# First attention of a fused two-layer kernel: batch 1's score shift, the scale transpose and the exponentials change places

## The reference

```python
x = x + L0_xattn(ln(x), ctx)    # 16 heads of 32, causal, softmax
x = x + L0_ffn(ln(x), ...)      # 8 experts, top 2, SiLU gating
x = x + L1_xattn(ln(x), ctx)    # 16 heads, low-rank queries, keys with rope
x = x + L1_ffn(ln(x), ...)      # weights and activations rounded to 8 bit
```

```python
scores = q @ k.T / sqrt(32); scores = where(causal, scores, min)
attn = softmax(scores); out = (attn @ v) @ Wout.T
```

## Time and profile before

| | value |
|---|---|
| median of 3 runs | 837.28 us |
| profiled execution, its span | 830.72 us, 828.9 us |
| PE, DVE, ACT, POOL busy, share of the span | 83%, 62%, 50%, 30% |
| mean granted TensorE clock | 0.932 of full speed |
| chain that ended last: PE, DVE, ACT, issue, DMA | 59%, 15%, 9%, 8%, 5% |

### The profile page before, as it was taken

One profiled execution on the slowest core, in us unless ns is written; L12 is line 12 of the kernel. 1 busy time (PEld: TensorE's weight loads), 2 busy tenths in 40 slices (PEclk: granted clock), 3 DMA queues, 4 the chain that ended last, 5 costly groups with the idle time before them and its releaser, 6 DMA issues.

```text
span 828.9 us, 13011 instructions
## 1 busy us (share of the span) xinstructions
PE 690.5 (83%) x4427; PEld 552.5 (67%) x4427; DVE 510.2 (62%) x1038; ACT 416.0 (50%) x777; POOL 247.3 (30%) x278
## 2 busy tenths in 40 slices
PE   0799999654999999992988988988988698799985
PEld 0587777453777777692867877878867375566542
DVE  4876677474666666538476476476475623677674
ACT  3513566363555555321377477476475522455452
POOL 2000742332122222054066166085073001122232
PEclk9987999765999999996799999999999999999997
DMA  8565842598675665698001223123257952111000
GB/s 260 192 209 145 297 147 59 185 390 302 188 228 176 188 184 162 206 297 202 12 1 50 60 50 85 42 60 77 64 172 201 387 191 70 52 52 39 13 14 28
DMA packets 82964, 118.90 MB, mean 143 GB/s; under 512 B 40769, under 2 KB 63037, under 8 KB 79329
## 3 DMA queue, kind: packets, MB, share of 16 engines
q1 hardware_dynamic: 79777, 109.71, 41.6%
q0 software_dynamic: 3136, 8.53, 4.1%
HBM read 97.15 MB, written 27.62 MB: 151 GB/s over the span
## 4 chain that ended last, share of the span: by engine, by line
PE 59%; DVE 15%; ACT 9%; issue 8%; DMA 5%; POOL 1%; ACTq 1%; SPq 0%; DVEq 0%; POOLq 0%
PE PS L149 14%; PE PS L151 12%; PE PS L150 12%; PE PS L1231 4%; PE PS L1407 3%; PE PS L1292 3%; PE PS L1589 2%; DMA raw<-wkv_in 2%; DMA yg<-ys_scratch,slots 2%; DVE nmx L1810 2%; ACT w_hi L884 1%; PE PS L1384 1%; ACT cx_hi L1119 1%; DMA cx_raw<-tile_scratch 1%; ACT wraw L973 1%
## 5 line engine op out<-in xcount | busy, mean ns | idle before, releaser
L831 POOL TENSOR_TENSOR wraw<-wraw,rinv 128x361 f32<-128x361 f32 (+1 forms) x104 | 80.9, 787 | 127.2 <-DVE rinv L1803 126.3
L1646 DVE TENSOR_TENSOR w_lo<-w,w_hi 128x1408 fp32r<-128x1408 f32 x40 | 64.9, 1623 | 39.7 <-ACT w_hi L884 39.7
L973 ACT ACTIVATE wraw<-PS,nmx 128x361 f32<-128x361 f32 (+1 forms) x104 | 58.6, 564 | 30.8 <-DVE nmx L1810 17.8
L1810 DVE TENSOR_REDUCE nmx<-PS 128x1 f32<-128x361 f32 (+1 forms) x104 | 55.1, 531 | 30.3 <-PE PS L151 30.3
L859 POOL TENSOR_TENSOR wraw<-gs,us 128x352 f32<-128x352 f32 (+1 forms) x28 | 26.7, 953 | 139.8 <-ACT gs L1147 112.2
L1813 DVE TENSOR_TENSOR pt_lo<-PS,pt_hi 128x384 fp32r<-128x384 f32 (+1 forms) x104 | 55.7, 535 | 16.3 <-ACT pt_hi L979 15.0
L884 ACT CAST w_hi<-w 128x1408 fp32r x40 | 54.7, 1369 | 18.6 <-DMA w<-w_in 9.4
L784 POOL DMA_INDIRECT xb<-xn_scratch,rows x20 | 31.8, 1589 | 106.6 <-PE PS L1203 103.5
L1407 PE MATMUL PS<-ident,wraw 128*128 128x128 f32 x312 | 52.2, 276 | 11.3 <-DVE pt_lo L1813 5.5
L149 PE MATMUL PS<-w_hi,xt_hi 128*128 128x352 f32 x160 | 56.9, 355 | 5.6 <-DVE xt_lo L1640 5.4
L149 PE MATMUL PS<-pf_hi,cx_hi 128*128 128x512 f32 (+1 forms) x112 | 48.1, 429 | 11.8 <-DVE x_tiles L2003 4.5
(11 more groups left out here) (270 smaller groups left out, 1937.1 us busy)
## 6 DMA issues: line engine op xcount, KB each, us to landing
w<-w_in SPq DMA_DIRECT2D x20, 768.0 KB, 5.5
w<-w_in SPq DMA_DIRECT2D x8, 1408.0 KB, 11.4
fq_raw<-foldq_in SPq DMA_DIRECT2D x6, 1088.0 KB, 7.8
cx_raw<-tile_scratch SPq DMA_DIRECT2D x6, 1024.0 KB, 5.1
ys_scratch<-yb SPq DMA_DIRECT2D x20, 256.0 KB, 5.5
ctx_scratch<-ctxo SPq DMA_DIRECT2D x24, 192.0 KB, 1.9
fp_raw<-foldp_in SPq DMA_DIRECT2D x7, 640.0 KB, 5.0
wraw<-wup_in SPq DMA_DIRECT2D x12, 256.0 KB, 4.3
```

Of the source, the lines that this page charges most:

```text
L831: pool.tensor_tensor(P1[slot][0:rows, 0:NK], P1[slot][0:rows, 0:NK], rinv[0:rows, jj, t:t + 1].broadcast_to((rows, NK)), ALU.mult).then_in ...
L973: act.activation(P1[t % 8][r, 0:NK], PS[r, t % 4, 0:NK], ACT.Exp, bias=nmx[r, jj, t:t + 1], accum_out=rsum[r, jj, t:t + 1]).then_inc(C["ex ...
L1646: dve.tensor_tensor(WL[which][:, :], w12_of(dve_wlo.e, which), WH[which][:, :].bitcast(F32), ALU.subtract) \
L1810: dve.tensor_reduce(nmx[r, jj, t:t + 1], PS[r, t % 4, 0:NK], AX.X, ALU.max, negate=True).then_inc(C["max"], 1)
```

## The change

There are three edits, all in the first attention's loop.

1. DVE takes the maxima of batch 1's scores and shifts them before `dve_maxima(7)`, `dve_maxima(8)` and `dve_scales()`, and no longer in `batch(0)`.
2. PE's `turn_scales` moves from `batch(0)`, ahead of pv(0), to `batch(1)`, behind ot(0) and ahead of pv(1). The wait for ACT's copy moves from the second half of pv(0) to that of pv(1), and ACT's copy `act_scale_rows` from `batch(0)` to `batch(1)`, behind `OH` of batch 0.
3. On ACT the exponentials of batch n+1 come ahead of `act_add(n-2)`, in every batch that has both (n = 2 to 6).

```diff
@@ ACT, batch(n, j)
                 if n > 0:
                     act_attn0_oh(act, n - 1)
-                else:
+                if n == 1:
                     act_scale_rows()
+                if n < B - 1:
+                    act_attn0_exp(act, n + 1, 1 - j)
                 if n >= LAG0:
                     act_add(n - LAG0)
-                if n < B - 1:
-                    act_attn0_exp(act, n + 1, 1 - j)
                 if n >= LAG0 and n % 2 == 0:
                     act_sub(n - LAG0)
@@ PE, pe_attn0_pv
-                if g == 1 and n == 0:
+                if g == 1 and n == 1:
                     pe.wait_ge(W["sc"], 4)
@@ PE, batch(n, j)
                 if not first:
                     pe_attn0_ot(pe, n - 1)
+                if n == 1:
+                    turn_scales()
                 if first:
                     pe.wait_ge(A["ksb"], 8)
-                    turn_scales()
                 pe_attn0_pv(pe, n, j)
@@ DVE
             dve_attn0_project(dve, 3 * MT0 + 3)
+            dve_attn0_max(dve, 1, 1)
+            dve_attn0_shift(dve, 1, 1)
             dve_maxima(7)
             dve_maxima(8)
             dve_scales()
@@ DVE, batch(n, j)
-                if not last:
+                if not last and not first:
                     dve_attn0_max(dve, n + 1, 1 - j)
                 if not first:
                     dve_attn0_low(dve, n - 1)
-                if not last:
+                if not last and not first:
                     dve_attn0_shift(dve, n + 1, 1 - j)
```

## The result

The changed kernel takes 843.76 us (median of 20 runs, 841.01 to 855.4), the kernel before beside it 837.9 us (median of 20, 833.93 to 846.05). Executions of one and the same kernel spread over 10 us and more, so single executions show where time goes inside a stage, and only ratios say what a kernel is worth. The profiled execution took 841.71 us, its span 839.9 us, against 830.72 and 828.9 before; the mean granted clock is 0.929 (0.932). That execution before lies 7.2 us under its kernel's median and under all 20 runs (the lowest took 833.93), the changed one 2.1 us under its own, so 11.0 us between the two profiles overstate the change.

A forecast was written before the change was run, and what follows sets the result against it. PE was taken to bound the stage, on a 10.26 us ring per batch. Terms -1.7, +1.6, +1.0, +1.2, +0.2 gave +2.3, another slow stretch (+1.6) made +3.9: 834.6 profiled, 841.2 median; range 835.0 to 846.0.

The forecast's parts named there:

- The clock swings: Rival, chance 0.20: uneven batches bring four slow stretches instead of two, or POOL starts at 95.7; + 7, 844.3 us.
- The opening: Edits 1 and 2, batch 0: pv(0) starts 1.7 us earlier, out(0) and all that follows 3.3 us earlier.
- idling and the slow stretch behind it: Opening: PE waits before pv(0), then runs at clock 0.50 from 71.94 to 82.18; edits 1 and 2 bear on this.
- the early-start rival: Rival, chance 0.17: full clock through the opening, lead 6.2, POOL at 90.2; -2.1, 835.2 us.
- POOL's start: Weights' chain behind the opening: POOL's first multiplication at 92.6 instead of 87.60, bounds 91.5 and 95.7.
- Of the 3.3 us, 1.7 are left: Batch 2: ACT's add waits for POOL's set 0, ready at 96.5, cutting the opening's lead to 1.7 us.
- An even batch is 1.0 us longer: Edit 3: ACT reaches the copy of group 0 1.58 us later, so group 3 is turned at 103.38, not 102.40.
- Batch 4: + 1.0: Edit 3's cost in batch 4, counted as + 1.0 us in the sum at the attention's end.
- The slow stretches: Two half-clock stretches behind PE's idle time, + 1.6 us each: one in batch 2 or 3, one with batches 4 and 6.
- batches 3 and 5 about 10.3: Sign to look for: these odd batches take about 10.3 us at full clock; + 0.2 us for both in the sum.
- the ring: A batch's lap in the first attention, 10.26 us: addition, PE's transposes and ACT's copy, scores, ot, pv, out, next addition.
- I carry it through at par: Behind the attention: layer norm, routing and expert loads start from its end, so its + 3.9 us passes on unchanged.

The follow-up runs named there:

- e5: Changed kernel, but POOL waits with set 3 until VectorE has rounded set 1, and exponentials come ahead of the add in batch 2 alone: 1.0029 to before.
- e4: Kernel before with edit 3 alone (exponentials ahead of the add): 1.0106 to before.
- e1: Changed kernel, but POOL waits with weight set 3 until VectorE has rounded set 1: 1.0094 to before.
- e11: Changed kernel with only set 1's weight load moved behind the store of the scale rows: 1.0083 to before.
- e9: Kernel before with edits 1 and 2, set 1's load behind the scale rows' store, POOL's set 3 waiting for VectorE's rounding of set 1: 0.9954 to before.
- e12: Kernel before with only set 1's weight load moved behind the store of the scale rows: 1.0000 to before.
- e10: e9 with edit 3 (exponentials ahead of the add) kept: 1.0047 to before.
- e8: Changed kernel with edit 3 undone and POOL waiting with set 3 until VectorE has rounded set 1: 1.0046 to before.
- e3: Changed kernel with edit 3 undone, the exponentials behind the add again: 1.0073 to before.
- e2: Kernel before with five unused multiplications put ahead of POOL's first set, making POOL late: 1.0054 to before.
- e7: Kernel before with edit 2 alone: 1.0017 to before.

## Why the prediction was right, and where it was wrong

- **Direction and size.** 841.2 was forecast from 837.28, 3.9 us slower; the medians beside each other are 5.9 us apart and the ratio says 0.8%. The time, 843.76, lies in the range, but just above the likeliest case's own (839 to 843.5), and nearer to the 844.3 of "The clock swings" than to the forecast. That rival isn't borne out for it: POOL started at 91.42 and not at 95.7, and behind the opening the profiled attention adds one slow stretch, in batch 3, and lengthens those of batches 6 and 7, where that rival has four.
- **The opening** (edits 1 and 2). Right: a lead of 3.3 us was forecast, batch 0's residual came 3.8 us earlier (openings of one code differ by over 2 us, as said under the table). DVE's order and PE's half clock from 71.7 went as written; the fall ended at 78.54, and a second followed from 82 to 85.5 (0.52), as before. But "idling and the slow stretch behind it" put the fall down to the idle time, and so did the early-start rival ("the idle 1.7 us before the slow stretch goes"): that idle time went, and the clock fell at 71.9 all the same.
- **POOL's start.** Forecast 92.6, measured 91.42, just under the bound of 91.5. The store's landing was right (83.6 against 84.10), the leg behind it 7.3 us instead of 8.93. This mattered: set 0 was ready at 95.32, just before ScalarE's add asked for it at 95.38. "Of the 3.3 us, 1.7 are left" is the term mis-sized by that; 2.9 were left (residual of batch 2, 110.63 to 107.69). With POOL one us later the wait that I had forecast is there, as e5 shows.
- **An even batch is 1.0 us longer.** Right for the wait at full clock: 11.10 against 10.26, 0.84, in batch 2, and e4 shows it without the other edits. "Batch 4: + 1.0" didn't come: batch 4 took 10.25, since ScalarE had caught up in the slow batch 3; e1 and e11, without a collision, paid in it (14.22 and 12.67).
- **The slow stretches.** Two were forecast at 1.6 us each. In the profiled execution one followed the collision in batch 3 (2.2 us), and batch 6 ran at clock 0.64. I had placed the first in batch 2, which kept clock 1.00. For batch 6, 1.2 and 1.6 were counted; batches 6 and 7 together lost 1.7, since the kernel before ran slowly there too.
- **What failed: "batches 3 and 5 about 10.3".** Batch 3 took 15.92. I had let POOL's run move against the ring and asked only who waits for POOL's results, not who shares something with POOL while it runs. VectorE's rounding of set 1 came at 111.96 before, 0.9 us behind POOL's last instruction; the lead of 2.9 us and POOL's delay of 3.8 pushed one into the other. No wait in the code joins them. Any lead of the opening is lost here, as the rounding ends with POOL's run however early it starts. Batch 3's own term was 0.1, and 3.5 us of TensorE's waiting and 2.2 of slow clock were measured. At the attention's end +3.9 was forecast and +4.4 measured, but the parts differ. The lead left after batch 2 was 2.9 and not 1.7, batch 3 with its slow stretch 5.7 and not 1.7, batch 4 nothing and not 1.0, batches 6 and 7 together 1.7 and not 2.8. That they come near the same total is luck.
- **The tail.** "I carry it through at par": the attention's end moved by 4.4 us and the profiled span by 11.0. The remaining 6.6 us lie behind the attention, where neither kernel differs, and all of it in the first feed-forward part: from the statistics of the first layer norm behind the attention to those of the next it took 230.9 us before (161.77 to 392.68, clock 0.90) and 238.0 changed (166.15 to 404.19, 0.88), and what follows took 0.5 us less. The same code took between 230.7 (e9, e12) and 245.1 us (e1) in the other kernels, so most of this can be the spread of executions; the medians are 5.9 apart, 1.5 more than the attention's 4.4. The runs don't settle which part belongs to the change.

So the cause, as far as it was taken apart: edit 3 costs about 1% in both places where it was added to a kernel without a late POOL and its collision (e4; e10 against e9). Edits 1 and 2 together, with POOL's wait on set 3, are a gain of 0.5% once POOL starts earlier (89.22 in e9, against 91.64 in e8, which differs by the load order alone), and are spent when it does not (e3, e5, e8 at 1.003 to 1.007). Losses don't add: the changed kernel has both and is at 1.008, and taking edit 3 out of it (e3) changed the ratio by less than its interval. Why they don't add the profiled batches suggest, the collision hiding batch 4's loss and a late POOL making batch 2 long without edit 3, but one execution of each is all there is.

## What to carry to other kernels

When a producer is moved, follow the whole chain that starts at it, here maxima, scales, a small store, a load, another engine's run, and ask of the last link both who waits for its results and what it runs beside in its new place. An instruction put ahead of another on a queue is only free if the idle time behind it is as long as that ahead of it: the add filled a wait of 2 us before the exponentials, and nothing behind them. And on this stage a wait of one to three us on TensorE can cost several, since the clock may go with it (e5's 2.87 us: a batch of 18.92 us).

## What the runs showed of the hardware

One VectorE instruction, a subtraction of a constant from 2432 fp32 elements in SBUF, cannot run beside POOL's multiplications. It took 1.41 us with POOL idle and 7.09, 5.57, 3.19 and 1.64 with POOL at work (changed, e2, e7, e3), each time ending 1.3 us after POOL's last instruction. In e7, VectorE and then POOL:

```profile
113.05 3.19 DVE L1858 TENSOR_SCALAR wraw<-raw_odd 128x2432 bf16<-128x2432 f32 x1
```

```profile
111.10 3.87 POOL L762 TENSOR_TENSOR raw_even<-raw_even,wraw 128x384 f32<-128x384 f32 x4
```

VectorE's other work in the same stretches kept its time (shift and maxima 2.00 and 2.02 us with POOL busy). The Trainium skill ("SBUF — State Buffer", section "🔬 SBUF: two separate sides") has a pair of ports shared by VectorE and GpSimd, taken as an exclusive lock by whichever comes first, for VectorE instructions that work in a two-port mode. The trace agrees, and shows that the lock was not passed on between POOL's instructions: in the changed kernel VectorE, from 109.02 on, waited through the rest of the run that the rows at 107.52 and 110.96 show (three and four instructions). In e11 it began at 107.58, inside a pause of 1 us between POOL's instructions, and took 1.41.

TensorE's clock fell to 1.2 GHz behind idle times of 1.7 us (before, ahead of 71.94) and 2.87 us (e5, batch 2 at 0.65), and not behind the 1.12 us in batch 2 of the changed kernel; it also fell in e4's batches 4 and 6 with the same added wait that batch 2 passed at 1.00. Nor does it need an idle time: in the changed kernel it fell at about 71.9, with TensorE at work without a pause since 68.58. What decides it, these runs don't show. The cost was 2.2 us (changed, batch 3) and more, and differs between executions of the same order: batch 2 took 11.10 us in the changed kernel and 13.01 in e1.
